# Moving on-chip staging traffic from the GpSimd queue to the SyncE queue in an eight-core attention and mixture-of-experts kernel

## What is computed

```python
q = (hidden @ Wq.T).reshape(b, s, H, D)      # H = D = 64, likewise k and v, each times a mask
scores = jnp.einsum('bshd,bsgd->bshg', q, k) / np.sqrt(D)
w = jax.nn.softmax(scores, axis=-1)
out = jnp.einsum('bshg,bsgd->bshd', w, v).reshape(b, s, HID) @ Wo.T

base = xf @ W_base.T + b_base                 # ffn
w = top-2 routing weights of xf @ W_router.T  # (T, 8)
lora = jnp.einsum('ter,te,eor->to', h, w, B) * SCALING
```

## Time and profile before

| | us |
|---|---|
| runs of the kernel (three) | 7796.50, 8145.56, 8429.89 |
| median of them | 8145.56 |
| the profiled execution | 7813.11 |
| its span on core 1 (other cores 7743.4 to 7793.1) | 7811.6 |

### The profile page before, as it was taken

How to read it: one execution, slowest core, us unless ns; L and a number is a source line. 1 busy time by engine, 2 the same in 40 slices (tenths; PEclk the granted TensorE clock), 3 DMA queues, 4 the chain that set the end, 5 groups by cost and what they waited for, 6 DMA issues and landing times.

```text
span 7811.6 us, 69961 instructions; the slowest of 8 cores (7743.4 to 7811.6 us)
## 1 busy us (share of the span) xinstructions
PE 5402.7 (69%) x28056; PEld 2545.8 (33%) x28056; DVE 1493.1 (19%) x2144; ACT 774.0 (10%) x1427; POOL 843.0 (11%) x1233
## 2 busy tenths in 40 slices
PE   4888888873455466564826999999933664767773
PEld 2333333333222233222313434444423332323331
DVE  4000000014222341301023000000033223322112
ACT  1000000003222210000001000000022222000000
POOL 1000000011211100111100000000021111000000
PEclk7999999985677678787967999999955886888887
DMA  5666766652477555788552222222223444555655
GB/s 143 143 145 144 143 145 144 143 117 57 101 164 163 150 185 174 187 185 231 173 203 104 87 86 84 86 84 84 81 66 76 119 110 141 185 193 154 207 177 191
DMA packets 540719, 1084.79 MB, mean 139 GB/s; under 512 B 182001, under 2 KB 374514, under 8 KB 524018
## 3 DMA queue, kind: packets, MB, share of 16 engines
q0 software_dynamic: 251472, 568.50, 32.1%
q1 hardware_dynamic: 288930, 511.82, 19.8%
HBM read 885.23 MB, written 369.10 MB: 161 GB/s over the span
## 4 chain that ended last, share of the span: by engine, by line
PE 61%; DMA 16%; DVE 11%; ACT 6%; issue 4%; POOL 2%; DVEq 0%; SPq 0%; ACTq 0%; POOLq 0%
PE PALL L341 35%; PE PALL L592 11%; PE PALL L765 8%; DVE BN L192 4%; DMA T<-yn 3%; DMA WG<-wbT 3%; ACT QBD L496 2%; DMA WG<-woT 2%; ACT PSTG L472 2%; PE PALL L278 1%; DMA T<-apn 1%; PE PALL L489 1%; PE PALL L409 1%; DVE QBD L418 1%; DMA qn<-QST 1%
## 5 line engine op out<-in xcount | busy, mean ns | idle before, releaser
L341 PE MATMUL PALL<-WG,LNT 128*128 128x512 bf16 x12288 | 2799.7, 387 | 262.3 <-DVE QST L359 173.4
L341 PEld LDWEIGHTS PALL<-WG,LNT 128*128 128x128 bf16 x12288 | 1215.1, 99 | 1846.4 <-issue 485.9
L592 PE MATMUL PALL<-WG,LNT 128*128 128x512 bf16 x4096 | 1039.1, 414 | 144.8 <-DMA WG<-woT 99.0
L765 PE MATMUL PALL<-WG,LNT 128*128 128x512 bf16 x4096 | 945.5, 392 | 128.4 <-DMA WG<-wbT 116.2
L278 PE MATMUL PALL<-idt,BFN 128*128 128x128 bf16 x1536 | 167.0, 306 | 831.4 <-DVE BFN L204 618.2
L592 PEld LDWEIGHTS PALL<-WG,LNT 128*128 128x128 bf16 x4096 | 419.2, 105 | 706.4 <-issue 332.7
L765 PEld LDWEIGHTS PALL<-WG,LNT 128*128 128x128 bf16 x4096 | 406.5, 100 | 654.3 <-issue 219.1
L192 DVE BATCH_NORM_STATS2 BN<-T 128x6 f32<-128x512 f32 x320 | 193.5, 676 | 1746.5 <-DMA T<-yn 1286.0
L359 DVE TENSOR_TENSOR QST<-PALL,maskK 128x512 bf16<-128x512 f32 x128 | 80.9, 685 | 1972.1 <-PE PALL L341 1915.4
L278 PEld LDWEIGHTS PALL<-idt,BFN 128*128 128x128 bf16 x1536 | 157.6, 144 | 846.4 <-issue 846.4
L437 ACT ACTIVATE KTS<-PALL 128x512 bf16<-128x512 f32 x192 | 104.2, 595 | 2705.9 <-PE PALL L429 2705.9
(11 more groups left out here) (105 smaller groups left out, 2460.5 us busy)
## 6 DMA issues: line engine op xcount, KB each, us to landing
WG<-s_wo SPq DMA_DIRECT2D x192, 512.0 KB, 3.4
WG<-s_wb SPq DMA_DIRECT2D x192, 512.0 KB, 3.7
XT<-x POOLq DMA_DIRECT2D x24, 2048.0 KB, 12.2
WG<-wqT POOLq DMA_DIRECT2D x64, 512.0 KB, 5.6
s_wq<-WG SPq DMA_DIRECT2D x64, 512.0 KB, 2.8
WG<-wkT POOLq DMA_DIRECT2D x64, 512.0 KB, 5.9
s_wk<-WG SPq DMA_DIRECT2D x64, 512.0 KB, 3.7
WG<-wvT POOLq DMA_DIRECT2D x64, 512.0 KB, 6.8
```

Source lines behind the costliest of these rows:

```text
L341: e.matmul(pb(tau, 0, 512), LNT[:, colk(kt, tau):colk(kt, tau) + 128], WG[b][:, k4 * 512:k4 * 512 + 512], start=st, stop=sp),
L592: e.matmul(pb(bk, 0, 512), LNT[:, colk(kt, tau):colk(kt, tau) + 128], WG[b][:, k4 * 512:k4 * 512 + 512], start=st, stop=sp),
L765: e.matmul(pb(bk, 0, 512), LNT[:, colk(kt, tau):colk(kt, tau) + 128], WG[b][:, k4 * 512:k4 * 512 + 512], start=st, stop=False), waits,
```

## The change

Four things are changed.

1. The `QST` stores of chunk 1 go from POOL to SP (line 366); chunk 0 had them there.
2. The eight loads of every attention batch (lines 382, 387 and 391) go from POOL to SP, in both chunks.
3. In the last call of `b6_units` (second half of chunk 1) the `XT` loads and the output stores go from POOL to SP, with semaphores of their own; the `T2` loads stay on POOL.
4. A last small memset on POOL waits for all output stores.

```diff
@@ -363,14 +364,12 @@
-                    qeng, qsn = ("sync", f"qs{sl}") if c == 0 else ("gpsimd", f"qsg{sl}")
-                    qv = dma(qeng, img[nm][tau * 128:tau * 128 + 128, 512 * n:512 * n + 512],
-                             QST[:, sl * 512:sl * 512 + 512], [(esem, ev)], sem=qsn)
-                    g_set(f"QSTs{sl}", (qsn, qv))
+                    qv = dma("sync", img[nm][tau * 128:tau * 128 + 128, 512 * n:512 * n + 512],
+                             QST[:, sl * 512:sl * 512 + 512], [(esem, ev)], sem=f"qs{sl}")
+                    g_set(f"QSTs{sl}", (f"qs{sl}", qv))
@@ -379,16 +378,16 @@
-                dma("gpsimd", dst, src, w_first + g_w(f"QSG{p}") if a == 0 else [], sem=f"rb{p}")
+                dma("sync", dst, src, w_first + g_w(f"QSG{p}") if a == 0 else [], sem=f"rb{p}")
...
-                    dma("gpsimd", dst, src, g_w(f"KB{p}") if (a == 0 and jp == 0) else [], sem=f"rb{p}")
+                    dma("sync", dst, src, g_w(f"KB{p}") if (a == 0 and jp == 0) else [], sem=f"rb{p}")
...
-                dma("gpsimd", dst, src, g_w(f"VB{p}") if a == 0 else [], sem=f"rb{p}")
+                dma("sync", dst, src, g_w(f"VB{p}") if a == 0 else [], sem=f"rb{p}")
@@ -801,28 +800,34 @@
-        def b6_units(taus, ywaits):
+        def b6_units(taus, ywaits, tailq=False):
+            qx = "sync" if tailq else "gpsimd"
+            xsem = "xls" if tailq else "xl"
+            osem = "outss" if tailq else "outs"
...
-                uq2 = dma("gpsimd", XT[:], xp_d[row0 + tau * 128: row0 + tau * 128 + 128, :],
-                          g_w("XT"), sem="xl")
+                uq2 = dma(qx, XT[:], xp_d[row0 + tau * 128: row0 + tau * 128 + 128, :],
+                          g_w("XT"), sem=xsem)
...
-                uq3 = dma("gpsimd", out_d[row0 + tau * 128: row0 + tau * 128 + 128, :], XT[:],
-                          [("V", v_)], sem="outs")
+                uq3 = dma(qx, out_d[row0 + tau * 128: row0 + tau * 128 + 128, :], XT[:],
+                          [("V", v_)], sem=osem)
...
-        b6_units(range(4, 8), b1h1_y)
+        b6_units(range(4, 8), b1h1_y, tailq=(c == NCH - 1))
...
+    emit("gpsimd", lambda e: e.memset(NHALF[:], -0.5),
+         [("outs", cnt["outs"]), ("outss", cnt["outss"])], inc="G")
```

More of the change, by code:

```diff
@@ L107, in _build_program @@
     DMASEMS = (["wg0", "wg1", "wg2", "wg3", "wgu0", "wgu1", "wgu2", "wgu3",
[1 row of a table removed]
+                "sw0", "sw1", "sw2", "sw3", "bbl0", "bbl1", "qs0", "qs1", "qs2", "qs3",
                 "rb0", "rb1", "ob0", "ob1", "onr", "xl", "t2l", "xps", "outs",
+                "xls", "outss",
                 "ap0", "ap1", "ap2", "ap3", "setq", "setu", "bfl0", "bfl1"])
@@ L365, in _build_program @@
                     g_set(f"bank{tau}", (esem, ev))
-                    qeng, qsn = ("sync", f"qs{sl}") if c == 0 else ("gpsimd", f"qsg{sl}")
-                    qv = dma(qeng, img[nm][tau * 128:tau * 128 + 128, 512 * n:512 * n + 512],
-                             QST[:, sl * 512:sl * 512 + 512], [(esem, ev)], sem=qsn)
-                    g_set(f"QSTs{sl}", (qsn, qv))
+                    qv = dma("sync", img[nm][tau * 128:tau * 128 + 128, 512 * n:512 * n + 512],
+                             QST[:, sl * 512:sl * 512 + 512], [(esem, ev)], sem=f"qs{sl}")
+                    g_set(f"QSTs{sl}", (f"qs{sl}", qv))
         g_set("LNTa", ("T", cnt["T"]))
         g_set("LNTb", ("T", cnt["T"]))
-        qpre = "qs" if c == 0 else "qsg"
-        a2_img_q = [(f"{qpre}{i}", cnt[f"{qpre}{i}"]) for i in range(4)]
+        a2_img_q = [(f"qs{i}", cnt[f"qs{i}"]) for i in range(4)]
         def attn_batch(tau, bt, wavesz, banks):
@@ L807, in b6_units @@
                           list(ywaits) + g_w("T2"), sem="t2l")
-                uq2 = dma("gpsimd", XT[:], xp_d[row0 + tau * 128: row0 + tau * 128 + 128, :],
-                          g_w("XT"), sem="xl")
+                uq2 = dma(qx, XT[:], xp_d[row0 + tau * 128: row0 + tau * 128 + 128, :],
+                          g_w("XT"), sem=xsem)
                 av = lnorm(T2[:], T2[:], [("t2l", uq1)])
                 v_ = emit("vector", lambda e: e.tensor_add(XT[:], XT[:], T2[:]),
-                          [("xl", uq2), ("V", av)], inc="V")
+                          [(xsem, uq2), ("V", av)], inc="V")
                 g_set("T2", ("V", v_))
-                uq3 = dma("gpsimd", out_d[row0 + tau * 128: row0 + tau * 128 + 128, :], XT[:],
-                          [("V", v_)], sem="outs")
-                g_set("XT", ("outs", uq3))
+                uq3 = dma(qx, out_d[row0 + tau * 128: row0 + tau * 128 + 128, :], XT[:],
+                          [("V", v_)], sem=osem)
+                g_set("XT", (osem, uq3))
         b6_units(range(0, 4), b1h0_y)
```

## The result

The changed kernel is slower: it takes 1.0591 times as long as the kernel before, 95% interval 1.0427 to 1.0756. Over all its nine runs the median is 8341.72 us (8206.37 to 8640.41), against 8098.87 us (7787.32 to 8429.89) for the ten runs of before. In some executions of either kernel the cores of one die run at a lower granted clock and take longer; the ratio leaves such executions out, and as the profiled one of the changed kernel is among them, core 1, on the undisturbed die, is read for both kernels from here on. The ratio rests on few runs: three of before, 7798.0 us on average, and two of the changed kernel, 8206.37 and 8311.96.

The account below looks back on a forecast made before the run. PE bounds the projections; a chain of small steps through PE, DVE and ACT bounds attention alone. 108 + 127 - 14 + 22 + 30 - 8 = +265 on 7813.1 us gives 8078 (+3.4%), range 7933 to 8350.

Parts of the forecast that it names:

- Part 1: Projections, chunk 1: next block's first weight load waits behind the stores on SP, 4.7 us at each of 23 ends, +108.
- clip at 4.7: Block ends, chunk 1 projections: at most 5.0 us more worked out, 4.7 taken, as chunk 0 blocks take 4.0 more.
- Part 2, second batches: Attention alone: loads wait behind the first batch's stores; start 14.2 us after its end, 15.9 later than now, +127 in all.
- dear reads: Rival, all 32 attention batches: 128-byte loads from SP run like `wrT`, 8.1 us more each, +259, 8337; chance 0.14.
- cheap rate: Attention loads, in the rival cheap order: 246 GB/s from SP, -2.6 us for each of 32 batches, -83.
- cheap order: Rival, whole kernel: attention loads at 246 GB/s and stores at their low price, +151 us, 7964; chance 0.16.
- Part 2, first batches: Attention alone, first batch after another `tau`: starts 17.7 us after the end instead of 20.0; six of -2.3, -14.
- Part 3, chunk 1: Attention between matmuls: second batches +24, first batches -10, late weight groups +8; +22 us.
- Part 3, chunk 0: Attention between matmuls: first batches +2 each, +8; three second batches 7.3 later each, +22; +30 us.
- Part 4: Tail: `T2` load no longer queues behind the output store, -8 us between bounds of 0 and 15; memset 0.
- POOL is the brake: Rival, faster: POOL's descriptor work holds up casting weight loads, PE waits 99.0 us; freeing it gives -103, 7710; chance 0.06.

## Why the prediction was right in direction and too small

The direction, the places and most of the mechanism were right. The sum was too small: +265 forecast, +400 by stages. The measured ratio, 1.0591, would be +461 on the profiled 7813, but it hangs on the higher of two runs; the lower gives +408. The step that failed is the price of part 3 in chunk 0, between matmuls: +2 for each first batch and 7.3 for three of the four second batches, +30 in all, where the stage lost 92. Part 1 and the first batches of part 2 were under-priced too.

- **Part 1, stores on SP: +108 forecast, +137 measured.** The wait for each next weight group, its place and the 23 ends are as forecast. PE was to start 9.4 us after a block's end and starts 10.4 after (mean of the 23 waits; the row shows 10.72). The stores went out when they should have (5.8 us after the end, inside 5.6 to 6.7), but the first weight load behind them took 4.1 us to land (median of the 23 ends), not the 3.3 of all such loads. Those are mostly issued one at a time, some 6 us apart. Here four are issued at once behind eight stores. The 256 matmuls took 57.7 us, near the forecast's 57.4: from block to block it is 68.1 us, less 10.4. The clip at 4.7 of a computed 5.0, argued from chunk 0, took the sum the wrong way. Measured was 6.3 from block to block, which is 144 us for 23 ends, less 3 for the last block, which has no end behind it.
- **Part 2, second batches: right.** 14.2 to 14.5 us after the end in chunk 1, forecast 14.2, with the loads at the rate of the stores. That the stage as a whole met +57 is in part luck: on core 1 it is +53. PE waited for `VB<-vn` 25 times and not 32, because between the matmuls of chunk 1 it mostly waits for weights instead. The window over the eight loads:

```profile
6029.50:6036.50 7.00, 0.00 (x0) 0.00 (x0) 0.00 (x0) 0.00 (x0) 0.00 (x0) 0.50 1.09 173
1763.00:1771.00 8.00, 0.00 (x0) 0.00 (x0) 0.00 (x0) 0.00 (x0) 0.00 (x0) 0.50 0.76 120
```

  173 GB/s against the 175 taken from the stores of a batch; dear reads and the cheap rate both fall. The second line is the same moment in chunk 0: 120 GB/s, with nothing else moving, and second batches there start 16.3 to 18.4 us after the end. That is 13 us of the +80 against +57, and the first batches below are 7 more. Why the same loads run slower in chunk 0 stays open: each piece took as long on its engine as in chunk 1, and the engines were busy 0.76 of the time instead of 1.09, so pieces came to them more slowly.

  The rate of the rival "cheap order", 246 GB/s, was misread. Its window holds the `BFN` load, 1049 of 1721 KB, in packets of 8 KB. The same batch's loads without it, a little later in the trace of the kernel before:

```profile
5771.00:5779.00 8.00, 3.57 (x32) 3.33 (x32) 2.77 (x4) 2.34 (x4) 4.34 (x5) 0.50 1.01 205
```

  So from POOL these loads run at 205 GB/s. The trace lists their packets with 4096 bytes, and those of the same loads from SP with 128. The rival's rate term would have been about -1.3 a batch and not -2.6; the comparison of 175 with 246 in "Dear reads" becomes one of 175 with 205.
- **Part 2, first batches:** forecast 17.7 us after the end, 2.3 less than the 20.0 of the earlier trace rows. Measured were 19.2 on average in chunk 1, against 20.7 before, and 21.8 in chunk 0, against 21.7: a gain of 1.5 each in one chunk and none in the other. The four `KB` loads hold SP for 7.17 us beside the `BFN` load (6075.17), where they take 3.64 without it.
- **Part 3, chunk 1: +22 forecast, +31 measured.** Second batches started at 24.2, 23.3 and 22.4 us against the 21 forecast, and the one put at 0 started 2.7 later. First batches came 2.6 to 4.2 sooner, forecast 2.5. Late weight loads are there (PE waits 59.3 us for them, 19.4 before), but the run with the weights ahead doesn't part their share from the lost cover.
- **Part 3, chunk 0: +30 forecast, +92 measured, the largest miss.** That the loads wait behind the store of the bf16 copy was seen, at the right place (16 us in the row). Its price was set at +2 a batch, because the loads from POOL landed late as well. It left out that the casting loads, which POOL issued one and then three around a batch's loads before (2227.73 and 2236.05), now leave four at once (2120.38) and run beside the batch's loads, which then take 24 us from first issue to L408, not 12. The four first batches started 13, 14, 7 and 5 us later than before: 39 instead of the forecast's 8. The second batches cost more still: 10, 18, 10 and 8 us later, 46 instead of 22, where the forecast took 1.2 for the casting loads beside them and put the first of the four at nothing.
- **Part 4, tail: -8 forecast, +3 measured.** Taken between bounds of 0 and 15, on the reading that the `T2` load stands behind the output store. It doesn't: it left 0.5 us after it in both kernels, and the last three of them landed in 11.8 to 12.4 us before and 12.3 to 12.5 after. The memset was put at 0, but the end comes 9.8 us after the last store has landed where it came 5.1 after. That is where the tail lost, against a gain of about 1.5 us ahead of it.

The rival "POOL is the brake" was wrong: POOL lost 351 us of its busy time (843 to 492), PE's wait for `WG<-woT` went from 99.0 to 87.3 us only, and with the same order attention alone took as long from SP as from POOL, or 9 us longer. The rule of the Trainium skill that stood on its side ("DMA: Bandwidth & Descriptors", Issuing engine by pattern) is not borne out for this traffic: once the order was equal, SP and POOL were within 4 us in attention alone of chunk 1, and SP was 9 us slower in chunk 0. Its line that spreading DMAs over the issuing engines doesn't help bandwidth (the same page, Rules for kernel authors) agrees with that.

## What to carry to other kernels

- A DMA with a wait is a gate on its queue's list. Before moving one, write down what stands behind it and how far ahead those were issued: here nearly all of the loss was prefetch that a waiting store had cut off, and a change of order alone took it back everywhere but between the matmuls of chunk 1.
- Two streams belong on one list only if the one that waits for compute comes after the one that feeds compute. If they can't be ordered so, keep them on two.
- Price a transfer in its new place by rows with the same company (issued behind others, or beside another queue's), not by the median over its quiet issues. Look, too, at what else a window holds before its rate is used.
- When an edit removes a wait, make the same edit in the kernel before. The weights ahead took 24 us off the changed kernel and 16 off the one before, so the 24 are not a measure of what the change had cost there.

## What the runs showed of the hardware that was not expected

- SP can be held in the act of issuing: four 128 KB loads in 128-byte pieces took 3.64 us to issue in a quiet stretch and 18.90 us beside four casting loads from POOL, and two 256 KB loads 3.13 and 9.41 us. The kernel before shows it already: two `on<-OB` stores held SP for 1.66 us in attention alone and for 12.51 us at 2143.71, between the matmuls of chunk 0. Everything behind them on SP's list is held too.
- Loads in 128-byte pieces from SP ran at 173 GB/s, the rate of stores in the same pieces, but at 120 GB/s in one chunk with nothing beside them. The cause was not found. From POOL the same loads ran at 205 GB/s, in packets of 4096 bytes instead of 128.
- The granted clock in the projections of chunk 1 fell from 0.97 to 0.93, with 10 us of idle at the end of each block in place of matmuls broken off for some 4. The 256 matmuls of a block took 57.7 us, where 57.4 had been worked out from the kernel before.
